# Order of work in the two-half attention rows and at the image turn of a four-layer convolution and attention kernel

## The reference, cut to what matters

```
x = x + L0(_gn(x))   # sign, 3x3 convolution with ternary weights
x = x + L1(_gn(x))   # rfft2, complex product per frequency, irfft2
x = x + L2(_gn(x))   # 7x7 convolution (64 to 64 channels) + bias
x = x + L3(_gn(x))   # attention in windows of 8x8 tokens, 8 heads:
                     #   q, k: relu, cubed, renormalised; linear attention;
                     #   + 5x5 depthwise convolution of v; projection
```

## Time and profile before

| | us |
|---|---|
| Median of three runs | 13394.39 |
| The profiled execution | 13400.7 |
| Its span | 13398.6 |
| TensorE busy (products) | 10752.5 (80%) |
| VectorE busy | 7732.4 (58%) |
| ScalarE busy | 6033.3 (45%) |
| GpSimd busy | 3730.8 (28%) |
| Mean granted TensorE clock | 0.887 |

### The profile page before, as it was taken

One profiled execution on the slowest core, in us unless ns is written; L12 is line 12 of the kernel. 1 busy time (PEld: TensorE's weight loads), 2 busy tenths in 40 slices (PEclk: granted clock), 3 DMA queues, 4 the chain that ended last, 5 costly groups with the idle time before them and its releaser, 6 DMA issues.

```text
span 13398.6 us, 290171 instructions
## 1 busy us (share of the span) xinstructions
PE 10752.5 (80%) x120871; PEld 9299.7 (69%) x120871; DVE 7732.4 (58%) x13708; ACT 6033.3 (45%) x7016; POOL 3730.8 (28%) x3112
## 2 busy tenths in 40 slices
PE   6888878848888888888888888877888888888886
PEld 4666668847777777777777777766777777776775
DVE  6666622245656666666566555666566666666665
ACT  4555521104444444444444444444444444444443
POOL 0000000003333333333333333333333333333332
PEclk9999988869988988988889889888899898989897
DMA  7888889941111111111111111111111111111100
GB/s 186 209 213 216 212 193 241 241 127 37 32 31 33 33 32 33 33 32 33 33 32 34 32 32 38 37 35 31 32 32 32 33 32 32 34 32 32 34 18 16
DMA packets 996827, 947.06 MB, mean 71 GB/s; under 512 B 591776, under 2 KB 936848, under 8 KB 979920
## 3 DMA queue, kind: packets, MB, share of 16 engines
q1 hardware_dynamic: 972048, 708.59, 24.5%
q0 software_dynamic: 23488, 220.21, 4.5%
HBM read 605.77 MB, written 322.96 MB: 69 GB/s over the span
## 4 chain that ended last, share of the span: by engine, by line
PE 45%; DVE 13%; issue 8%; POOL 6%; ACT 4%; DMA 2%; DVEq 0%; SPq 0%; POOLq 0%; ACTq 0%
PE c_ps L922 28%; PE c_ps L989 3%; PE c_ps L1062 3%; PE c_ps L1049 3%; POOL c_xr L1546 3%; PE c_ps L1020 2%; POOL c_xr L1550 2%; DVE c_v L1383 2%; DVE c_qt L1413 2%; DVE c_qt L1421 2%; DVE c_xr L1365 2%; PE c_ps L1002 2%; DVE c_xr L1302 1%; ACT c_qt L1182 1%; PE c_ps L1041 1%
## 5 line engine op out<-in xcount | busy, mean ns | idle before, releaser
L922 PE MATMUL c_ps<-c_xp,c_wst 128*128 128x224 f16 x45696 | 5060.2, 270 | 345.0 <-DVE c_xp L1347 345.0
L922 PEld LDWEIGHTS c_ps<-c_xp,c_wst 128*128 128x128 f16 x45696 | 4466.3, 100 | 1005.0 <-issue 692.7
L1546 POOL TENSOR_TENSOR c_xr<-c_sm,c_xr 128x448 f32<-128x448 f32 x448 | 751.4, 1677 | 3761.3 <-DVE c_xr L1365 3761.3
L1174 ACT ACTIVATE c_bs<-c_ps,c_unscale 128x448 f32<-128x448 f32 x224 | 141.7, 633 | 3127.9 <-POOL c_xr L1550 3093.6
L1571 POOL TENSOR_TENSOR c_cube<-c_sq,c_qk 128x896 f32<-128x896 f32 x448 | 925.9, 2088 | 845.7 <-ACT c_sq L1206 845.7
L1020 PE MATMUL c_ps<-c_qt,c_wproj 64*64 64x448 f32 x1792 | 370.7, 912 | 979.8 <-ACT c_qt L1182 979.8
L1140 ACT ACTIVATE c_tn<-c_xr,c_nrm 64x448 f32<-64x448 f32 (+1 forms) x960 | 1099.3, 1145 | 116.5 <-DVE c_xp L1347 101.7
L1442 DVE TENSOR_REDUCE c_s<-c_sq 128x28 f32<-128x1792 f32 x224 | 452.5, 2020 | 1141.1 <-ACT c_sq L1206 1141.1
L989 PE MATMUL c_ps<-c_wqkv,c_xn 64*128 64x192 f32 x6272 | 819.9, 377 | 173.0 <-DVE c_v L1383 165.5
L528 PE MATMUL b_ps<-b_xs,b_wt 64*64 64x64 f32 x6384 | 795.3, 299 | 172.1 <-DVE b_xj L504 162.4
L1379 DVE TENSOR_TENSOR c_qk<-c_ps,c_bqk 128x512 f32<-128x512 f32 (+1 forms) x896 | 557.8, 623 | 597.2 <-PE c_ps L989 596.8
(11 more groups left out here) (155 smaller groups left out, 18046.2 us busy)
## 6 DMA issues: line engine op xcount, KB each, us to landing
b_wt<-in_L_conv_weight SPq DMA_DIRECT2D x56, 2048.0 KB, 22.1
a_xc<-in_x SPq DMA_DIRECT2D x64, 1568.0 KB, 18.9
x<-a_x1s POOLq DMA_DIRECT2D x32, 3136.0 KB, 22.8
a_xh<-x SPq DMA_DIRECT2D x64, 1568.0 KB
c_xr<-x SPq DMA_DIRECT2D x224, 448.0 KB, 4.1
out<-c_xr SPq DMA_DIRECT2D x448, 224.0 KB, 3.1
xf<-a_freq POOLq DMA_DIRECT2D x32, 1792.0 KB, 17.6
b_xs<-xf SPq DMA_DIRECT2D x28, 2048.0 KB, 26.0
```

The lines of the kernel that those rows point to most:

```text
L922: ins = pe.matmul(sums(c, p), wst[:, ws, pr, FIRST_TAP[p] + k].rearrange("p q o -> p (q o)"), xp[:, xs, PLANE[kind] + f, row:row + CROWS, ...
L1546: pool.tensor_tensor(here, apart(sm[:, half]).unsqueeze(1).to_broadcast([P, 2, CROWS, QW]), here, ALU.add).then_inc(s.added, 1)
```

## The change

The order of instructions changes at six places, and two semaphores are new.

- ScalarE, attention row: `turned` and the square come before the first `take_b`.
- VectorE, attention row: the folds of sums 6 and 7 of the chunk before stand between `divide` and the second `take_qkv`, the fold of sum 8 after it.
- TensorE and ScalarE, turn: `turn_back` and `turned` move from c1 group 4 to 8, `give_back` and `give` from 8 to 12.
- x1: the last stripe has a semaphore of its own, and VectorE waits for it at chunk 12 of the c2 additions.
- First four chunks of planes: VectorE pads one half of the image with `tensor_scalar` (`padded_low`), ScalarE the other; the zeros of chunk 0 are written before the norm is known.
- Chunk 0 of the convolution starts with the products that need the first two chunks of planes; `start` is set once for each bank; projections 2 and 3 of row 0 move from the turn into the row.

```
+ORDER = [(p, i) for p in range(NP) for i in range(12 * PRODUCTS[p][2])]
+FIRST_ORDER = sorted(ORDER, key=lambda o: o[0] < NP - 1 and o[1] >= 3 * PRODUCTS[o[0]][2] or 2 * (o[0] == NP - 1))
+HALF_ROWS = ((slice(0, C), slice(C, P), 2), (slice(C, P), slice(0, C), 1))
-FIRST_PIECES = (0, 0, 0, 0, 0, 100, 188)
+FIRST_PIECES = (0, 40, 0, 64, 0, 150, 188)
...
+        x1_end = [sem("x1_end0"), sem("x1_end1")]
...
-                             ).then_inc(x1_in[odd], 16)
+                             ).then_inc((x1_in if a < A7 - 1 else x1_end)[odd], 16)
...
# TensorE, conv_some
+                    p, i = FIRST_ORDER[i] if c == 0 else ORDER[i]
...
-                            pe.wait_ge(s.lo_done, n * NCH + min(2 * c + 3, NCH))
+                            pe.wait_ge(s.lo_done, n * NCH + (2 if c == 0 else min(2 * c + 3, NCH)))
...
+                    elif c == 0 and p == 0 and i == 3 * taps:
+                        pe.wait_ge(s.lo_done, n * NCH + 3)
...
-                                    start=(i == 0), stop=(i == 12 * taps - 1), skip_group_check=True)
+                                    start=(i == 0 and p % 2 == 0), stop=(i == 12 * taps - 1), skip_group_check=True)
...
# TensorE, bring (ScalarE's bring has the same two numbers)
-                        if g == 4:
+                        if g == 8:
                             turn_back(row - 1)
-                        if g == 8:
+                        if g == 12:
                             give_back(row - 1)
...
                 if above_zero(n):
-                    for g in range(1, 4):
-                        project(row, g)
+                    project(row, 1)
...
# TensorE, attend, for a == 0
+                else:
+                    conv(pieces[1])
+                    project(l, 2)
+                    conv(pieces[3])
+                    project(l, 3)
                 conv(pieces[5])
...
# ScalarE, bring
+                zero_rows(0, HALF_ROWS)
                 deviation(2 * n)
                 act.wait_ge(s.rstd_done, 2 * n + 1)
-                for k in range(EARLY):
-                    padded_chunk(n, odd, k)
-                    if k:
-                        high_part(n, k - 1)
-                high_part(n, EARLY - 1)
+                padded_chunk(n, odd, 0)
+                padded_chunk(n, odd, 1)
+                high_part(n, 0)
+                high_part(n, 1)
+                padded_chunk(n, odd, 2)
+                padded_chunk(n, odd, 3)
+                high_part(n, 2)
+                high_part(n, 3)
...
# ScalarE, padded_chunk: one half of the image where k < EARLY
+                halves = HALF_ROWS[0:1] if k < EARLY else HALF_ROWS
...
# ScalarE, attend
                 pad()
-                conv(True)
                 if a:
                     turned(l - 1)
...
                 act.activation(sq[:], qk[:], ACT.Square).then_inc(s.u2_done, 1)
+                conv(True)
                 if a:
                     give(l - 1)
...
# VectorE, bring
-                dve.wait_ge(x1_in[odd], 8 * A7 * (n + (2 - odd)))
+                dve.wait_ge(x1_in[odd], 8 * (A7 - 1) * (n + (2 - odd)))
                 for c in range(CHUNKS):
+                    if c == 2 * (A7 - 1):
+                        dve.wait_ge(x1_end[odd], 8 * (n + (2 - odd)))
...
+                padded_low(n, odd, 0)
+                padded_low(n, odd, 1)
+                qkv(0)
+                differ(n, 0)
+                differ(n, 1)
+                low_part(n, 0)
+                padded_low(n, odd, 2)
+                low_part(n, 1)
+                padded_low(n, odd, 3)
+                qkv(1)
+                differ(n, 2)
+                low_part(n, 2)
+                qkv(2)
+                differ(n, 3)
+                low_part(n, 3)
+                qkv(3)
...
+            def padded_low(n, odd, k):
...
+                dve.tensor_scalar(pad_put(k)[to, :, a - lo:b - lo], pad_get(odd)[of, :, a - first:b - first],
+                                  nrm[of, 0, 0:1], nrm[of, 0, 1:2], ALU.mult, ALU.add).then_inc(s.normed_low, 1)
...
# VectorE, attend
                     take_qkv(l, 0)
                     divide(l - 1)
+                    conv_before(6)
+                    conv_before(7)
                     take_qkv(l, 1)
+                    conv_before(8)
                     multiply(l - 1)
                     take_qkv(l, 2)
                     add_depthwise(l - 1)
                     take_qkv(l, 3)
                     relu(l)
-                conv_before(6)
-                conv_before(7)
-                conv_before(8)
...
# GpSimd, differ
+                if k < EARLY:
+                    pool.wait_ge(s.normed_low, n * EARLY + (k + 1))
+                    pool.nop(nofuse=True)
```

More of the change, by code:

```diff
@@ L1082, in last @@
                 stats(2 * n - 1, 1)
-                for g in range(4):
+                for g in range(2):
                     project(row, g)
@@ L1117, in bring, with zero_rows @@
                     window_rows((n - 1) * A7, 0, 1 - odd)
+                if above_zero(n * NCH - 1):
+                    act.wait_ge(s.lo_done, n * NCH - 1)
+                zero_rows(0, HALF_ROWS)
                 deviation(2 * n)
                 act.wait_ge(s.rstd_done, 2 * n + 1)
-                for k in range(EARLY):
-                    padded_chunk(n, odd, k)
-                    if k:
-                        high_part(n, k - 1)
-                high_part(n, EARLY - 1)
+                padded_chunk(n, odd, 0)
[6 more added lines that the diff above has]
+                high_part(n, 3)
+            def zero_rows(k, halves):
+                lo, hi = spans[k]
+                for to, of, first in halves:
+                    a, b = max(lo, first), min(hi, J + first)
+                    for row in [*range(lo, a), *range(b, hi)]:
+                        act.activation(pad_put(k)[to, :, row - lo:row - lo + 1],
+                                       ident[of, 0:W].rearrange("p (r j i) -> p r j i", r=4, j=1), ACT.Copy, scale=0.0)
             def padded_chunk(n, odd, k):
@@ L1131, in padded_chunk @@
                     act.wait_ge(s.lo_done, n * NCH + (k - 1))
[L1133 to L1136, removed]
+                halves = HALF_ROWS[0:1] if k < EARLY else HALF_ROWS
+                if k:
+                    zero_rows(k, halves)
+                for to, of, first in halves:
                     a, b = max(lo, first), min(hi, J + first)
[L1138 to L1141, removed]
+                    ins = act.activation(pad_put(k)[to, :, a - lo:b - lo], pad_get(odd)[of, :, a - first:b - first],
+                                         ACT.Identity, scale=nrm[of, 0, 0:1], bias=nrm[of, 0, 1:2])
                 ins.then_inc(s.normed, 1)
@@ L1308, in bring @@
                 row = (n - 1) * A7
-                if above_zero(n):
-                    take_qkv(row, 0)
-                    take_qkv(row, 1)
-                differ(n, 0)
-                if above_zero(n):
-                    take_qkv(row, 2)
-                low_part(n, 0)
-                differ(n, 1)
-                if above_zero(n):
-                    take_qkv(row, 3)
-                    relu(row)
-                low_part(n, 1)
-                for k in range(2, EARLY):
-                    differ(n, k)
-                    low_part(n, k)
+                qkv = lambda g: take_qkv(row, g) if above_zero(n) else None
+                padded_low(n, odd, 0)
[14 more added lines that the diff above has]
+                qkv(3)
+                if above_zero(n):
+                    relu(row)
+            def padded_low(n, odd, k):
+                lo, hi = spans[k]
+                to, of, first = HALF_ROWS[1]
+                a, b = max(lo, first), min(hi, J + first)
+                if k < 2:
+                    dve.wait_ge(s.rstd_done, 2 * n + 1)
+                    if above_zero(n * NCH - 1 + k):
+                        dve.wait_ge(s.lo_done, n * NCH - 1 + k)
+                else:
+                    dve.wait_ge(s.lo_done, n * NCH + (k - 1))
+                dve.tensor_scalar(pad_put(k)[to, :, a - lo:b - lo], pad_get(odd)[of, :, a - first:b - first],
+                                  nrm[of, 0, 0:1], nrm[of, 0, 1:2], ALU.mult, ALU.add).then_inc(s.normed_low, 1)
             def x2_stats(n, odd, c):
```

12 lines of the change are left out of this document (7 added, 5 removed).

## The result

The changed kernel takes 11986.66 us (median of 4 runs, 11974.22 to 11995.25) against 13385.53 us (4 runs) for the kernel before: ratio 0.8953, 95% interval 0.8937 to 0.8968. The forecast was 11,990. Its profiled execution took 11989.07 us, 1412 us less than that of before (span 11987.4); TensorE is busy 87% of it, and the mean granted clock rose from 0.887 to 0.926.

What follows compares the result with a forecast made beforehand. ScalarE's queue was taken to bound the kernel: turned, needed by TensorE, stood behind the first take_b, which waited for GpSimd's adds. Gains 1153 + 111 + 140 = 1404 us from 13400.7 gave 11,990 us; range 11,820 to 12,340.

Steps and rivals of the forecast that it cites:

- The stall and the clock, rows 1 to 6: Attention rows 1 to 6: the stall before the give-back goes and the clock recovers; 6.2 us a row, 1153 us.
- the excess of 0.6: Rows 1 to 6: time beyond TensorE's own 31.25 us from the serial chain to the mask; middle of 0 to 1.2.
- Fold 8 and the held add: Rows 1 to 6: later third folding makes TensorE wait 0.45 us; add_depthwise, if held by GpSimd's adds, 0.9 us late.
- R1: Rival, chance 0.16: GpSimd's moved adds hold add_depthwise and relu; row 34 us, gain 953 us, time 12,440 us.
- This needs both halves: Rows 1 to 6: x3_done ahead of the first take_b needs (a) and (b); with (a) alone adds end at +16.5.
- (a): ScalarE, rows 1 to 6: turned and square go ahead of first take_b, so the give-back, due at +12.5, doesn't wait.
- (b): VectorE, rows 1 to 6: folds 6 and 7 fill a 1.11 us gap at no cost; fold 8 delays what follows by 0.55.
- (e): Turn, VectorE: last x1 stripe awaited only at c = 12, so the wait moves to load 5; with (d), 111 us.
- load 5: Turn: x1 load of the stripe before the last, forecast to land some 3 us before the last stripe's load.
- (d): Turn, TensorE and ScalarE: turned and give move from c1 groups 4 and 8 to 8 and 12; with (e), 111 us.
- the kind of turn with the long wait: The 17 turns where the turn-back waited 4.28 us: forecast gain 5.8 us each, against 0.9 in the other 14.
- (f): First planes after the norm: halved pads, early zeros, TensorE starting on two chunks; 4.5 us an image, 140 us, bounds 0 and 211.

Runs made afterwards that it cites:

- run with three edits: Changed kernel with earlier x1 loads, fold 8 behind the third projection's folding, and ScalarE's old row order (first take_b ahead of turned): 12,435.85 us, ratio 0.9286.

## Why the prediction was right, and where not

The time was 3 us off, and the main mechanism held; so close a hit is luck. By its steps, for an image:

- **The stall and the clock, rows 1 to 6: right.** Forecast 6.2 us a row and 37.2 an image; measured 5 x 6.49 + 5.85 = 38.3. TensorE's own work, 31.25, was the row (31.32 where no mask is waited for). Of the excess of 0.6 only 0.35 came, most of it the wait of 0.6 us for the mask in two of five rows. The clock was a second price, as worked out: over the rows of the kernel before the stall was 5.2 us, the give-back 0.8 us and the 40 products 1.0 us longer than after (1.76 and 0.98; 5.16 and 4.14).
- **Fold 8 and the held add: right.** The fourth projection waits 0.32 us (forecast 0.45). `add_depthwise` is held 0.93 us (forecast 0.9) and ends at +9.9 (+10.0). So R1 failed because only one instruction is held, not because nothing is: the relu starts when the adds are over. The Trainium skill (SBUF — State Buffer, "Who interferes with whom") lets a VectorE instruction with two SBUF inputs and a GpSimd one that reads SBUF exclude each other. The held `add_depthwise` (2.01 us for 1.08) agrees, and so do the adds and the relu in the run with three edits.
- **"This needs both halves": wrong.** VectorE's folds alone do it all. The prediction followed (a) without (b) to its late adds (the expectation of that run made 35 us of it; 33.18 measured), and never (b) without (a). With the folds early, `x3_done` comes before the turn-back ends, whatever ScalarE's order. What ScalarE's order brings is a margin: it pays when `x3_done` is late, and costs 0.2 us a row where it is not.
- **(e) The wait moves to load 5: right.** The waits for x1 are 114.1 us after, 114.4 before, over 28 images each, and go when load 5 is early. (d) and (e) together gave 4.89 - 0.38 = 4.5 us an image, 3.6 forecast. From c1 to the norm's product the kind of turn with the long wait gained 5.9 us (5.8 forecast), the other 3.0, not 0.9: "hardly waited" was read from one turn, and over 13 turns of that kind the turn-back had waited 0.98 to 4.45 us, 2.75 on average.
- **(f) First planes: mechanism right, term mis-sized.** 4.5 us forecast, 9.55 - 6.90 = 2.65 measured by the timelines, 59 us of 140 by the run without it. In the image shown the start came at +8.9 (+8.2 forecast), and projection 3 ended at +19.1 (+17.5): the first 40 products begin at 0.50 clock and take 6.28 us. So the relu ended at +23.2 (+21.7), the first cube at +28.4 (+26.4) and the mask at +42.7 (+41.3). The stall at the key-values was forecast (2.7 us, 2.26 measured), but not that the clock falls behind it. That makes 1.14 us more in 26 of 31 images, 0.96 an image. The start gained 9.55 us, where 10.0 was forecast. The two together are 1.4 of the 1.85 us that are missing. And row 1 waits for the mask, as forecast, only in the other 5 images.
- The error of +1.1 us in the rows, +0.9 in (d) and (e) and -1.85 in (f) cancel; the exact hit is luck, within a range that the terms bear.

## What to carry to other kernels

When an engine stands for a copy that is queued behind another wait, look for what makes that other wait late, and try moving that alone: here the producer's order (VectorE) removed the stall for all rows, and the consumer's order only adds a margin. Don't add up edits measured apart when they share a wait: late fold and old order were each harmless or better, and together made the kernel 450 us slower than the changed one. Idle time in front of an instruction is not what its releaser costs. It can be more: 4.75 us of waits for x1 gave 2.3 when the load was early, because the next condition, TensorE's c2 products, stood close behind. On TensorE it can be less: 5.2 us of stall came with 1.8 us of slow products behind it. And look at all images before calling a slow stretch free: where a stall moves, the slow clock can move with it.

## What the runs showed of the hardware that I had not expected

The length of a stall of TensorE did not by itself tell whether the clock would fall to 0.50 (1.2 GHz) behind it. By the work behind the stall:

| stall, us | where | slow behind it |
|---|---|---|
| 4.8 to 5.7 | before the give-back, kernel before | 186 of 186 rows |
| 2.61 to 2.66 | before the give-back, run with three edits | 76 of 186 rows |
| 2.26 | before the key-values, changed kernel | 26 of 31 images |
| 2.1 | before the numerators, eight products moved ahead | 16 of 31 images |
| 1.48 | before the key-values, the same run | 0 of 31 images |

The stall of 2.26 us was the same to 0.02 us in seven other runs and in them the key-values were slow in 16 to 27 of 31 images. What decides it no run here shows.

In the run with three edits GpSimd and VectorE held each other both ways: an add of 1.36 us took 2.95, and the relu of 2.03 took 2.48.
